# An attention block with experts on one core: scores in runs of three half tiles, values after one or two whole tiles

## The chip, the cores and the metric

The kernel runs on one core of one Trainium2 chip. The metric is the device time in microseconds of one execution of the whole program. Three runs of the kernel before gave 1203.56, 1205.45 and 1205.55 us; the median is 1205.45.

## The reference

Two sequences of 2048 tokens with 512 features go through causal attention with 16 query heads of 32 features that share one key head and one value head, a residual with a layer norm, a layer of eight experts of which each token takes two, and a second residual with a layer norm. The part that the change touches is this:

```python
qkv = jnp.einsum('bsd,ed->bse', x, Wqkv_w) + Wqkv_b
scores = jnp.einsum('bqhd,bkd->bhqk', q, k) * scale
scores = jnp.where(causal[None, None], scores, min_val)
attn = jax.nn.softmax(scores, axis=-1)
ctx = jnp.einsum('bhqk,bkd->bqhd', attn, v)
```

## The kernel before

The program loops over the two sequences. Each is worked in four stages g of four blocks q of 128 queries (q0 to q3, q4 to q7, q8 to q11, q12 to q15). A stage is attention, then the output product and the projections of the next stage, then the router and the experts.

A tile is one block of 128 queries against one block of 128 keys for all 16 heads, 2048 columns. Block q has q + 1 tiles, the diagonal one first, so a sequence has 136 tiles, numbered through (`TILES`, `FIRST[q]`, `LAST[q]`). Each engine has its own written order; semaphores join them:

- TensorE makes the scores of a tile in two halves of 1024 columns, two matmuls each (L1059). A half takes one of three places of a ring in PSUM. The fourth use of the ring takes the first place again and waits (`ring_free`) until the exponential has read the half that stood there, or, where a denominator stood there, until VectorE has transposed it (L798).
- ScalarE takes the exponential of each half into one of five buffers `prob` (L583). Before it writes a buffer again, it waits for the values and the addition, or the denominators, that read it.
- GpSimd masks the diagonal tile (L460). The first addition of a block waits for it.
- VectorE adds the tiles of a block up in `psum_k` (L749). The diagonal tile is taken in with the first addition; the last tile of q1 to q9 and the last two of q10 to q15 are left to TensorE (`BY_PE`); q0 and q1 have no addition.
- TensorE multiplies a tile's probabilities with the values (L1081, `times_values`): four column groups, two passes each, so eight passes, to a bank of PSUM that gathers the block. This is issued two tiles behind the scores (`LAG`).
- TensorE sums the rows of `psum_k` and of the tiles left to it into denominators (L1099, `denominators`), eight passes for each source: 24 passes where two tiles are left to it, 16 where one is. They are issued at the third tile of the next block (`DLAG`) and take a place of the ring. VectorE then transposes them (L798), takes reciprocals (L800) and scales the context (`normalise_context`).

In a stage but the first, the second half of the experts of the stage before (`finish_experts`, L1213 on TensorE, L822 to L832 on VectorE) comes behind the first tile's scores. VectorE starts its additions only behind that. Before the change the loop `attend_tiles` goes tile by tile: two halves of scores, then one tile's values, then denominators that are due. The list `ring_of` repeats this order, to give each use its place.

Behind the attention of a stage TensorE makes the output product (L949).

Of the kernel before, what the change touches and what calls it, by code (L numbers as in the profile page):

```python
# [35 lines left out]
P = 128  # L36
# [6 lines left out]
NG = S // BT  # L43
DC = D // P
TB = BT // P
NQ = S // P
HC = P // HD
HJ = H // HC
# [4 lines left out]
LAG = 2  # L53
# [7 lines left out]
FIRST = [TILES.index((q, q)) for q in range(NQ)]  # L61
LAST = [FIRST[q] + q for q in range(NQ)]
# [9 lines left out]
PV_ORDER = [t for q in range(NQ) for t in  # L72
            ([FIRST[q] + 1, FIRST[q]] + list(range(FIRST[q] + 2, LAST[q] + 1)) if q % TB
             else range(FIRST[q], LAST[q] + 1))]


def denominators_at(t):

    return [q for q in range(NQ) if LAST[q] + DLAG == t]


def ring_of(g):


    uses = []
    for t in range(FIRST[TB * g], LAST[TB * g + TB - 1] + 1):
        uses += [("scores", 2 * t), ("scores", 2 * t + 1)]
        uses += [("den", q) for q in denominators_at(t) if q >= TB * g]
    return uses


# [1 line left out]
RING_AT = [{use: n for n, use in enumerate(RING[g])} for g in range(NG)]  # L93
# [18 lines left out]
def build(nc, xT, x, wqkvT, bq, bvk, owT, ob, rT, w1, w2, w3, out):  # L112
    ctx = ExitStack()
    with ctx:
# [199 lines left out]
        def count(b, s, n):  # L314

            assert n > 0, (s, n)
            return b * GAIN[s] + n
# [15 lines left out]
        def score_half(g, u):  # L333

            return sc[:, RING_AT[g]["scores", u] % 3, :, :]
# [608 lines left out]
        def _(pe):  # L944
# [70 lines left out]
            with pe.Fori(0, B) as b:  # L1015
# [18 lines left out]
                def ring_free(g, n):  # L1034

                    if n >= 3:
                        kind, i = RING[g][n - 3]
                        if kind == "scores":
                            pe.wait_ge(exped, count(b, exped, i + 1))
                        else:  # L1040
                            pe.wait_ge(rden_ready, count(b, rden_ready, i + 1))

                def scores(t, g, shift):
                    q, k = TILES[t]
                    slot, at = (q % TB) // 2, (q % 2) * P
                    for half in range(2):
                        u = 2 * t + half
                        at_ring = RING_AT[g]["scores", u]
                        ring_free(g, at_ring)
                        if at_ring == 2:  # L1050
                            with pe.If(b > 0) if g == 0 else nullcontext():
                                pe.wait_ge(resid2, count(b - (g == 0), resid2, TB * ((g - 1) % NG) + (2 if g else TB)))
                                pe.sem_inc(waited_apart, 1)
                        for m in range(2):
                            c = 2 * half + m
                            if t == FIRST[q] and q % 2 == 0:
                                pe.wait_ge(stack_in[slot][c], count(b, stack_in[slot][c], 64 * (g + 1)))
                            dst = score_half(g, u)[:, m, :]
                            last = nc.tensor.matmul(dst, k_st[:, k * P:(k + 1) * P],  # L1059
                                                    q_st[slot][:, c * HJ:(c + 1) * HJ, at:at + P],  # L1060
                                                    start=True, stop=not shift)
                            for j in range(HJ if shift else 0):
                                h = c * HJ + j
                                last = nc.tensor.matmul(dst[:, j * P:(j + 1) * P],
                                                        minus_max[:, q % TB, h:h + 1].broadcast_to([P, P]),
                                                        ident[:, :], start=False, stop=(j == HJ - 1))
                        last.then_inc(scored, 1)

                def times_values(t):

                    q, k = TILES[t]
                    pe.wait_ge(exped, count(b, exped, 2 * (t + 1)))
                    if t == FIRST[q]:
                        pe.wait_ge(masked, count(b, masked, 2 * (q + 1)))
                    if t == PV_ORDER[FIRST[q]]:
                        if q % TB >= 2 or q // TB == 0 and q >= 2:
                            pe.wait_ge(ctx_out, count(b, ctx_out, q - 1))
                        elif q >= TB:
                            pe.wait_ge(resid2, count(b, resid2, TB * (q // TB - 1) + 3 + q % 2))
                    for c in range(HC):  # L1080
                        last = nc.tensor.matmul(top[q % 2][c * HD:(c + 1) * HD, :], v_sb[:, k, :],  # L1081
                                                prob[t % NP][:, c * BT:(c + 1) * BT],
                                                start=(t == PV_ORDER[FIRST[q]]), stop=(t == PV_ORDER[LAST[q]]))
                    last.then_inc(pv_done, 1)

                def denominators(q):

                    if FIRST[q] + 1 in ADDED:
                        pe.wait_ge(add_v, count(b, add_v, adds_until(LAST[q])))
                    if q % TB == TB - 1:  # L1090
                        pe.wait_ge(ctx_out, count(b, ctx_out, q))
                    else:
                        ring_free(q // TB, RING_AT[q // TB]["den", q])
                    parts = [prob[t % NP] for t in range(FIRST[q], LAST[q] + 1) if left_to_pe(t)]
                    if FIRST[q] + 1 in ADDED:
                        parts.append(psum_k[q % 2])
                    for n, src in enumerate(parts):
                        for c in range(HC):
                            last = nc.tensor.matmul(den_bank(q)[c * HD:(c + 1) * HD, :], ones[:, :],  # L1099
                                                    src[:, c * BT:(c + 1) * BT],  # L1100
                                                    start=(n == 0), stop=(n == len(parts) - 1))
                    last.then_inc(summed, 1)
# [14 lines left out]

                def attend_tiles(g, shift):
                    t0, t1 = FIRST[TB * g], LAST[TB * g + TB - 1]
                    for t in range(t0, t1 + 1):  # L1120
                        scores(t, g, shift)
                        if t == t0 and g:
                            finish_experts(g - 1)
                        if t - LAG >= t0:
                            times_values(PV_ORDER[t - LAG])
                        for q in denominators_at(t):
                            if q >= TB * g:
                                denominators(q)
                    for t in range(t1 - LAG + 1, t1 + 1):
                        times_values(PV_ORDER[t])  # L1130

# [164 lines left out]
```

## Time and profile before

| | us |
|---|---|
| median of three runs | 1205.45 |
| the profiled execution, its own time | 1201.47 |
| its span | 1199.3 |
| attention of the last stage of the first sequence, first score to last value | 424.0 to 561.5 |
| TensorE busy | 1099.2 |
| VectorE busy | 890.6 |
| ScalarE busy | 712.2 |
| mean granted TensorE clock, share of full | 0.978 |

The span is 2.2 us shorter than the profiled execution's time; the rest lies around it. Times of a row count from the span's start. PE is TensorE's matmuls, PEld its weight loads, DVE is VectorE, ACT ScalarE, POOL GpSimd. Busy shares are means over stages that have different limits, so a change is read from the stage that it is in.

### The profile page before, as it was taken

The page shows a single profiled execution, that of the slowest core. Times are in us where ns is not written, and L with a number is a line of the kernel's source. Part 1 is how long each engine was busy: PE and PEld are TensorE (multiplying, and loading weights), DVE is VectorE, ACT ScalarE, POOL GpSimd, SP SyncE. Part 2 cuts the span into 40 slices and gives each one's busy share as a digit, 9 for nine tenths or more (in the row PEclk, how much of TensorE's full clock was granted, in tenths as well). Part 3 has the DMA queues.
Part 4 walks back from the last instruction along what each step waited for, and adds up shares of the span by engine and source line. Part 5 has one row for each costly group of instructions (what it writes and reads, how often), then busy time and mean ns, then how long its engine had stood idle before and what let it go on. Part 6 is the DMA issues. An engine that isn't in the chain of part 4 may idle for free.

```text
span 1199.3 us, 18340 instructions
## 1 busy us (share of the span) xinstructions
PE 1099.2 (92%) x6080; PEld 525.2 (44%) x6080; DVE 890.6 (74%) x1095; ACT 712.2 (59%) x828; POOL 165.8 (14%) x153
## 2 busy tenths in 40 slices
PE   5489999998999999999989999999999999999976
PEld 4237433743335543333733743364333464333342
DVE  3176688669887589888677667875988767988856
ACT  4354568337884477887336347834688446788721
POOL 1250121102001012001004003020200101200000
PEclk9599999999999999999999999999999999999998
DMA  3991530063001432000154164016310143200000
GB/s 121 216 156 44 121 97 2 36 142 106 1 1 37 105 108 36 2 1 4 49 130 106 44 133 106 2 36 142 89 18 1 37 87 91 36 1 1 2 1 36
DMA packets 65678, 74.37 MB, mean 62 GB/s; under 512 B 14224, under 2 KB 48016, under 8 KB 65552
## 3 DMA queue, kind: packets, MB, share of 16 engines
q1 hardware_dynamic: 49968, 58.74, 19.0%
q0 software_dynamic: 13584, 11.54, 6.5%
q10 hardware_dynamic: 2000, 2.51, 0.7%
q8 instruction: 68, 1.11, 0.4%
q14 instruction: 58, 0.48, 0.1%
HBM read 25.58 MB, written 8.39 MB: 28 GB/s over the span
## 4 chain that ended last, share of the span: by engine, by line
PE 61%; DVE 22%; issue 8%; POOL 3%; ACT 2%; SPq 2%; DMA 1%; DVEq 0%; ACTq 0%; POOLq 0%
PE sc L1059 15%; DVE psum_k L749 13%; PE bank L1081 12%; PE sc L949 9%; PE sc L1198 7%; PE bank L949 7%; PE sc L1213 2%; PE sc L1099 2%; SPq L364 2%; ACT prob L583 2%; DVE stats L825 2%; PE bank L1099 2%; POOL prob L460 1%; DVE res L822 1%; PE sc L1144 1%
## 5 line engine op out<-in xcount | busy, mean ns | idle before, releaser
L583 ACT ACTIVATE prob<-sc 128x1024 f32<-128x1024 f32 x544 | 525.2, 1026 | 157.1 <-PE sc L1059 144.6
L749 DVE TENSOR_TENSOR psum_k<-psum_k,prob 128x2048 f32<-128x2048 f32 x170 | 395.6, 2327 | 5.1
L1059 PE MATMUL sc<-q_st,k_st 128*128 128x512 f32 x1088 | 334.0, 428 | 32.3 <-DMA q_st<-q_lo 11.7
L1059 PEld LDWEIGHTS sc<-q_st,k_st 128*128 128x128 f32 x1088 | 186.3, 191 | 280.2 <-ACT prob L583 178.3
L1081 PE MATMUL bank<-prob,v_sb 128*32 128x512 f32 x2176 | 290.7, 611 | 0.0
L460 POOL TENSOR_SCALAR_AFFINE_SELECT prob<-prob 128x1024 f32<-128x1024 f32 x64 | 88.7, 1423 | 596.5 <-ACT prob L583 596.5
L1198 PE MATMUL sc<-prob,w_sb 128*128 128x512 bf16 x512 | 123.0, 384 | 2.9 <-DVE prob L898 2.9
L749 DVE TENSOR_TENSOR psum_k<-prob 128x2048 f32<-128x2048 f32 x28 | 64.1, 2290 | 55.0 <-ACT prob L583 41.9
L1081 PEld LDWEIGHTS bank<-prob,v_sb 128*32 128x32 f32 x2176 | 44.0, 108 | 106.3 <-issue 90.7
L949 PE MATMUL bank<-q_st,wq_hi 128*128 128x512 f32 x240 | 81.0, 402 | 0.0
L615 ACT ACTIVATE prob<-sc 128x512 f32<-128x512 f32 x64 | 37.3, 597 | 69.8 <-PE sc L1198 69.7
L1198 PEld LDWEIGHTS sc<-prob,w_sb 128*128 128x128 bf16 x512 | 46.4, 99 | 66.3 <-issue 14.6
L949 PE MATMUL sc<-ow_hi,q_hi 128*128 128x512 f32 x128 | 52.3, 408 | 20.6 <-issue 20.6
L595 ACT ACTIVATE q_hi<-ctxn 128x512 fp32r<-128x512 f32 x32 | 20.3, 638 | 73.3 <-DVE ctxn L808 73.3
L817 DVE TENSOR_TENSOR q_lo<-ctxn,q_hi 128x512 fp32r<-128x512 f32 x32 | 50.6, 1590 | 12.3 <-ACT q_hi L595 12.1
L502 POOL TENSOR_TENSOR q_st<-res,q_st 128x2048 fp32r<-128x2048 f32 x7 | 33.1, 4733 | 144.0 <-ACT q_st L600 144.0
L898 DVE TENSOR_TENSOR prob<-sc,prob 128x512 f32<-128x512 f32 x64 | 42.1, 676 | 13.2 <-ACT prob L615 13.1
L949 PE MATMUL sc<-ow_lo,q_hi 128*128 128x512 f32 x128 | 50.6, 395 | 0.0
L949 PE MATMUL sc<-ow_hi,q_lo 128*128 128x512 f32 x128 | 50.6, 395 | 0.0
L949 PEld LDWEIGHTS bank<-q_st,wq_hi 128*128 128x128 f32 x240 | 45.7, 190 | 10.0 <-issue 0.2
L909 DVE TENSOR_TENSOR psum_k<-bank,prob 128x512 bf16<-128x512 f32 x64 | 42.4, 684 | 8.8 <-PE bank L1206 8.3
L545 ACT ACTIVATE q_hi<-bank,bq_sb 128x512 fp32r<-128x512 f32 x30 | 20.6, 689 | 45.9 <-PE bank L949 45.9
(127 smaller groups left out, 1004.9 us busy)
## 6 DMA issues: line engine op xcount, KB each, us to landing
q_st<-q_hi SPq DMA_DIRECT2D x128, 128.0 KB, 2.7
q_st<-q_lo SPq DMA_DIRECT2D x128, 128.0 KB, 2.7
res<-in_x SPq DMA_DIRECT2D x8, 1024.0 KB, 5.2
res<-ob_sb POOLq DMA_DIRECT2D x8, 1024.0 KB, 8.1
out_x<-res SPq DMA_DIRECT2D x32, 256.0 KB, 2.0
res<-in_xT SPq DMA_DIRECT2D x7, 1024.0 KB, 5.0
w_sb<-in_w POOLq DMA_DIRECT2D x8, 256.0 KB, 11.3
prob<-in_wqkvT ACTq DMA_DIRECT2D x4, 288.0 KB, 5.8
```

The source lines that it names most:

```text
L460: nc.gpsimd.affine_select(out=tile, in_=tile, compare_op=ALU.is_ge, fill=0.0, base=0, pattern=[[0, H // 2], [1, P]], channel_multiplier=-1 ...
L583: nc.scalar.activation(prob[t % NP][:, half * HW:(half + 1) * HW], score_half(q // TB, 2 * t + half).rearrange("p m n -> p (m n)"), ACT.Ex ...
L615: nc.scalar.activation(silu[e % 4], LOW[2 * (e % 3)], ACT.Silu).then_inc(silu_done, 1)
L749: nc.vector.tensor_tensor(acc[:, :], first[:, :], prob[t % NP][:, :], ALU.add).then_inc(add_v, 1)
L817: nc.vector.tensor_tensor(ctx_lo[:, :, toks], ctxn[:, :, toks], ctx_hi[:, :, toks].bitcast(F32), ALU.subtract).then_inc(ctx_low, 1)
L898: nc.vector.tensor_tensor(prod[e % 4], LOW[2 * (e % 3) + 1], silu[e % 4], ALU.mult).then_inc(prod_done, 1)
L909: nc.vector.tensor_tensor(hT[:, e, :], gate_bank(e)[:, :], prod[e % 4], ALU.mult).then_inc(h_done, 1)
L949: last = nc.tensor.matmul(dst, stationary[i][:, c, cols], moving[j][:, c, :], start=(c == 0 and n == 0), stop=(c == DC - 1 and n == 2))
L1059: last = nc.tensor.matmul(dst, k_st[:, k * P:(k + 1) * P], q_st[slot][:, c * HJ:(c + 1) * HJ, at:at + P], start=True, stop=not shift)
L1081: last = nc.tensor.matmul(top[q % 2][c * HD:(c + 1) * HD, :], v_sb[:, k, :], prob[t % NP][:, c * BT:(c + 1) * BT], start=(t == PV_ORDER[FI ...
L1099: last = nc.tensor.matmul(den_bank(q)[c * HD:(c + 1) * HD, :], ones[:, :], src[:, c * BT:(c + 1) * BT], start=(n == 0), stop=(n == len(par ...
L1198: last = nc.tensor.matmul(LOW[2 * (e % 3) + n], w[:, e, c, :], x1Tb[:, c, :], start=(c == 0), stop=(c == DC - 1))
```

## The change

TensorE's order in attention is the only thing that changes. The first tile of a stage is made as before. From then on scores are issued in runs of three halves. Behind a run come the values (two tiles behind, as before) and the due denominators of those tiles whose second half was made since the last run: one tile and two tiles in turn. The ring's list is made in the same new order. The same instructions run as before, as many of each, and the other engines' code is unchanged. From the second stage on, values of tiles t0 and later begin behind eight halves in place of six.

```diff
+def halves_of(g):
+    return range(2 * FIRST[TB * g], 2 * LAST[TB * g + TB - 1] + 2)
+
+def scored_by(g, u):
+    first, last = halves_of(g)[0], halves_of(g)[-1]
+    if u == first + 1:
+        return [u // 2]
+    if u != last and (u - first - 1) % 3:
+        return []
+    begin = first + 2 + 3 * ((u - first - 2) // 3)
+    return range((begin + 1) // 2 if begin % 2 == 0 else begin // 2, (u + 1) // 2)
+
 def ring_of(g):
     uses = []
-    for t in range(FIRST[TB * g], LAST[TB * g + TB - 1] + 1):
-        uses += [("scores", 2 * t), ("scores", 2 * t + 1)]
-        uses += [("den", q) for q in denominators_at(t) if q >= TB * g]
+    for u in halves_of(g):
+        uses.append(("scores", u))
+        uses += [("den", q) for t in scored_by(g, u) for q in denominators_at(t) if q >= TB * g]
     return uses
...
-                def scores(t, g, shift):
+                def scores(u, g, shift):
+                    t, half = divmod(u, 2)
                     q, k = TILES[t]
...
-                    for t in range(t0, t1 + 1):
-                        scores(t, g, shift)
-                        if t == t0 and g:
+                    for u in halves_of(g):
+                        scores(u, g, shift)
+                        if u == 2 * t0 + 1 and g:
                             finish_experts(g - 1)
-                        if t - LAG >= t0:
-                            times_values(PV_ORDER[t - LAG])
-                        for q in denominators_at(t):
-                            if q >= TB * g:
-                                denominators(q)
+                        for t in scored_by(g, u):
+                            if t - LAG >= t0:
+                                times_values(PV_ORDER[t - LAG])
+                            for q in denominators_at(t):
+                                if q >= TB * g:
+                                    denominators(q)
                     for t in range(t1 - LAG + 1, t1 + 1):
                         times_values(PV_ORDER[t])
```

Written out for q14 (tiles 105 to 119; s is a half, V a tile's values, D a block's denominators, | the end of a run):

```
before  s214 s215 V106 D13 | s216 s217 V105 | s218 s219 V107 | s220 s221 V108
after   s215 s216 s217 V106 D13 V105 | s218 s219 s220 V107 | s221 s222 s223 V108 V109
```

and for the start of q13 (tiles 91 to 104):

```
before  s186 s187 V92 D12 | s188 s189 V91 | s190 s191 V93
after   s185 s186 s187 V90 V92 D12 | s188 s189 s190 V91 | s191 s192 s193 V93 V94
```

## Rows read from the trace of the kernel before

**Rows 1.** The page: busy times; the chain that ended last; additions (busy us, mean ns).

```profile
PE 1099.2 (92%) x6080; PEld 525.2 (44%) x6080; DVE 890.6 (74%) x1095; ACT 712.2 (59%) x828; POOL 165.8 (14%) x153
...
PE 61%; DVE 22%; issue 8%; POOL 3%; ACT 2%; SPq 2%; DMA 1%; DVEq 0%; ACTq 0%; POOLq 0%
...
L749 DVE TENSOR_TENSOR psum_k<-psum_k,prob 128x2048 f32<-128x2048 f32 x170 | 395.6, 2327 | 5.1
```

**Rows 2.** Timeline, steady in q14: start us, duration us, engine, instructions [idle before <- releaser].

```profile
506.08 0.76 PEld L1059 LDWEIGHTS sc<-q_st,k_st 128*128 128x128 f32 x4 [0.84 <-ACT prob L583]
506.08 1.20 PE L1059 MATMUL sc<-q_st,k_st 128*128 128x512 f32 x4
506.85 1.94 ACT L583 ACTIVATE prob<-sc 128x1024 f32<-128x1024 f32 x2 [0.18 <-PE sc L1059]
...
507.21 1.07 PE L1081 MATMUL bank<-prob,v_sb 128*32 128x512 f32 x8
508.20 1.20 PE L1059 MATMUL sc<-q_st,k_st 128*128 128x512 f32 x4
508.97 1.02 ACT L583 ACTIVATE prob<-sc 128x1024 f32<-128x1024 f32 x1 [0.18 <-PE sc L1059]
```

**Rows 3.** Timeline of the same tile in windows so narrow that single starts show.

```profile
506.42 0.86 PE L1059 MATMUL sc<-q_st,k_st 128*128 128x512 f32 x3
...
506.88 0.40 PE L1059 MATMUL sc<-q_st,k_st 128*128 128x512 f32 x1
...
507.66 0.61 PE L1081 MATMUL bank<-prob,v_sb 128*32 128x512 f32 x4
```

**Rows 4.** Timeline, q12: exponentials back to back, and a score that waits for one.

```profile
439.56 1.94 ACT L583 ACTIVATE prob<-sc 128x1024 f32<-128x1024 f32 x2 [1.44 <-DVE psum_k L749]
...
440.64 0.50 PE L1059 MATMUL sc<-q_st,k_st 128*128 128x512 f32 x1 [0.25 <-ACT prob L583]
```

**Rows 5.** Timeline, the denominators of q13 at the third tile of q14.

```profile
493.66 2.29 DVE L749 TENSOR_TENSOR psum_k<-prob 128x2048 f32<-128x2048 f32 x1 [3.61 <-ACT prob L583]
494.01 1.06 PE L1081 MATMUL bank<-prob,v_sb 128*32 128x512 f32 x8
...
496.61 1.04 PE L1099 MATMUL sc<-psum_k,ones 128*32 128x512 f32 x8
...
497.58 0.77 PEld L1059 LDWEIGHTS sc<-q_st,k_st 128*128 128x128 f32 x4 [0.84 <-issue]
```

**Rows 6.** Waits for the transpose: waits view (us, times, longest); timeline behind q4, q9, q12.

```profile
PEld sc L1059 <- DVE rden L798: 28.3, 19, 3.1
...
163.29 1.89 PE L1059 MATMUL sc<-q_st,k_st 128*128 128x512 f32 x4 [2.19 <-DVE rden L798]
...
166.98 1.20 PE L1059 MATMUL sc<-q_st,k_st 128*128 128x512 f32 x4
...
322.41 1.21 PE L1059 MATMUL sc<-q_st,k_st 128*128 128x512 f32 x4 [0.41 <-DVE rden L798]
...
467.44 1.20 PE L1059 MATMUL sc<-q_st,k_st 128*128 128x512 f32 x4 [1.26 <-DVE rden L798]
```

**Rows 7.** Timeline, first stage: the second sequence's first six halves; the first sequence's DMA wait.

```profile
626.68 4.76 PE L1059 MATMUL sc<-q_st,k_st 128*128 128x512 f32 x12 [3.00 <-issue]
...
45.90 1.82 PE L1081 MATMUL bank<-prob,v_sb 128*32 128x512 f32 x8
...
53.33 0.76 PE L1059 MATMUL sc<-q_st,k_st 128*128 128x512 f32 x1 [4.95 <-DMA q_st<-q_lo]
```

**Rows 8.** Windows: busy PE, PEld, DVE, ACT, POOL, PEclk, DMA; then q15's end, timeline.

```profile
163.30:167.00 3.70, 3.70 (x13) 1.18 (x13) 3.54 (x4) 1.94 (x2) 0.00 (x0) 0.54 0.62 106
...
564.00:567.70 3.70, 3.70 (x20) 2.41 (x24) 3.70 (x1) 0.00 (x0) 3.44 (x1) 1.00 0.02 4
...
558.56 2.92 PE L1081 MATMUL bank<-prob,v_sb 128*32 128x512 f32 x24
...
563.95 0.49 PE L949 MATMUL sc<-ow_hi,q_hi 128*128 128x512 f32 x1 [2.46 <-issue]
```

More of the change, by code:

```diff
@@ L1041, in ring_free @@
                             pe.wait_ge(rden_ready, count(b, rden_ready, i + 1))
-                def scores(t, g, shift):
+                def scores(u, g, shift):
+                    t, half = divmod(u, 2)
                     q, k = TILES[t]
                     slot, at = (q % TB) // 2, (q % 2) * P
[L1046 to L1067, printed above, removed]
@@ new lines, in scores @@
+                    at_ring = RING_AT[g]["scores", u]
+                    ring_free(g, at_ring)
+                    if at_ring == 2:
+                        with pe.If(b > 0) if g == 0 else nullcontext():
+                            pe.wait_ge(resid2, count(b - (g == 0), resid2, TB * ((g - 1) % NG) + (2 if g else TB)))
+                            pe.sem_inc(waited_apart, 1)
+                    for m in range(2):
+                        c = 2 * half + m
+                        if t == FIRST[q] and q % 2 == 0:
+                            pe.wait_ge(stack_in[slot][c], count(b, stack_in[slot][c], 64 * (g + 1)))
+                        dst = score_half(g, u)[:, m, :]
+                        last = nc.tensor.matmul(dst, k_st[:, k * P:(k + 1) * P],
+                                                q_st[slot][:, c * HJ:(c + 1) * HJ, at:at + P],
+                                                start=True, stop=not shift)
+                        for j in range(HJ if shift else 0):
+                            h = c * HJ + j
+                            last = nc.tensor.matmul(dst[:, j * P:(j + 1) * P],
+                                                    minus_max[:, q % TB, h:h + 1].broadcast_to([P, P]),
+                                                    ident[:, :], start=False, stop=(j == HJ - 1))
@@ L1069, in times_values @@
+                    last.then_inc(scored, 1)
                 def times_values(t):
```

## The prediction

> **What bounds the kernel now.** I read the page's shares first, then the chain that ended last, then a steady stretch of the attention loop, then every place where that rhythm breaks. TensorE is busy for 92% of the span and holds 61% of the chain; VectorE 22% [rows 1]. In a steady stretch each tile (four score matmuls L1059, then eight value passes L1081) takes 2.12 us, 506.08 to 508.20. ScalarE needs 1.94 us for the tile's two exponentials and idles 0.18 waiting for scores; an addition takes VectorE 2.33 us, but not every tile has one [rows 1, 2]. So here TensorE sets the pace, with ScalarE 9% behind it.
>
> Inside the tile single instructions start so: scores 506.08, 506.42, then two more until 506.88; values 507.21, 507.66; next score 508.20 [rows 2, 3]. Neighbours of one kind follow after 0.23 us (scores) and, in a long train, 0.43 us for each four passes of values or denominators: eight last 1.04, four 0.61, and 8 value passes with 24 of the denominators take 494.01 to 497.58, which is 7 x 0.43 + 0.54 [rows 3, 5]. A change of kind costs more: 0.33 before the values instead of 0.23, 0.54 before the scores instead of 0.43, 0.34 for the second score instead of 0.23, 0.32 in all (with the 0.02 that the first value group takes beyond the rest). This is what the change addresses.
>
> Where TensorE waits in attention it waits mostly for VectorE: the third use of the ring behind a denominator needs the transpose L798 (28.3 us in the weight-load column, 19 times, longest 3.1). At 163.29 it waited 2.19, at 322.41 0.41, at 467.44 1.26 [rows 6]. Such places I call pins: VectorE (with GpSimd's masks ahead of it) sets their time.
>
> **The change part by part.**
> *Removed: switches.* No instruction is added or taken away. A pair of runs is six halves, that is three tiles: before 3 x 2.12 = 6.36 us, now 12 score matmuls, values of three tiles and two changes of kind, 6.36 - 0.32 = 6.04. All 136 tiles of a sequence go from 128 groups (after the first three tiles of each stage) to 85, so 43 switches x 0.32 x 2 = 28 us would go if nothing else ended late. That is the far end of the gain, not what I expect.
>
> *Added: waits inside a run.* The ring has three places, so the third half of a run needs the exponential of the third half of the run before. An exponential lasts 1.02 and two back to back 1.94, so they start 0.92 apart [rows 2, 4]. At 440.64 a blocked score starts 0.05 behind the end of the first of such a pair (439.56 + 1.02), and lasts 0.50 as the first behind a change of kind does, not 0.40, since its weights could not be loaded ahead [rows 4]. Take a run that starts at T after two tiles' values. Its first exponential starts at T + 0.77 (as 506.08 to 506.85), its third ends at T + 0.77 + 1.84 + 1.02 = 3.63. The next run (one tile's values between) starts at T + 2.58: 0.34 + 4 x 0.23 to the last score, 0.33 to the values, 0.99 through them. Its third half would start 1.03 later, T + 3.61, and may at T + 3.68. It is late by 0.07, and the lost preloading adds 0.1: about 0.15 a pair, taken once, because the run after two tiles' values has 0.8 us to spare. Net 0.32 - 0.15 = 0.17 for three tiles. The stall is a difference of two long sums, so I bound it by 0 and 0.3.
>
> *Moved: the denominators against the scores.* Behind q10, q13 and q14 the denominators now come after the first tile that reuses a buffer they read (two tiles are left to TensorE there), so its exponential waits for them. Before, its scores were issued behind them. If the last group of four passes starts at D, it ends at D + 0.61 (two such groups take 1.04 [rows 5]), the exponential at D + 1.66, and the scores that need its ring place may start at D + 1.71. Only one tile's values stand between, and they would let them start at D + 0.43 + 0.43 + 0.54 = 1.40: late by 0.3. The next half comes 0.57 later where its exponential takes 0.92 more: 0.35, and 0.1 for the lost preloading. That is some 0.73 each. For q1 (two tiles, both left to TensorE) the same. Bounds 0.3 to 1.0.
>
> *Moved: values behind a pin.* At a pin the time is VectorE's. Before, two halves of scores and one tile's values stood between denominator and pin; now three halves follow one another where the denominator ends its slot (q4, q5, q9, q12), and the values stand behind the pin. They were free in the idle time; they now cost 0.87 once for each last pin of a stage.
>
> The sum for one sequence, counted from the last pin of each stage (what is won before it is given back there):
> - q12 to q15: 41 tiles behind 467.44. The law above gives 41 x 2.12 + 2 x 2.6 for two denominators + 1.9 for the last two tiles' values = 94.0 us, the trace 558.56 + 2.92 - 467.44 = 94.0 [rows 6, 8]. 13.7 switches x 0.32 = -4.4; 11.7 waits x 0.15 = +1.8; two denominators +1.5; values behind the pin +0.9. Sum -0.2 to -0.4, I take -0.3.
> - q8 to q11: 19 tiles behind 322.41: -2.0, +0.8, one denominator +0.7, values +0.9: +0.4; the masks start a little earlier, I take +0.3.
> - q4 to q7: 11 tiles behind q5's denominator: -1.2, +0.5; the values behind it 0.87 less half a tile of scores already made (0.46): +0.4. Sum -0.3.
> - q0 to q3: beyond the third, the halves ahead of the first values are paced by exponentials: six take 4.76 us [rows 7], where free ones would take 3.0; two more such halves at 0.92, then two tiles' values: +0.3. One denominator +0.7, one wait +0.15, two switches -0.65. Sum +0.6.
> Together +0.3; two sequences +0.6. In the first sequence the scores of q2 wait for the stacked queries until 53.33, and the first values (1.82 us at the lower clock, 45.90) filled that time [rows 7]. They now stand behind it. A pin later in that stage can take most of it back: I take +0.4, bounds 0 and 1.8. Forecast +1.0 us: the profiled execution 1201.5 goes to 1202.5; on the median, 1206.5. About 0.2% (2.4 us) is what a measurement of this kernel can tell from no change.
>
> What hides the rest: the exponentials' later or earlier ends reach VectorE only where it idles (3.61 us before 493.66 [rows 5]); if that cover were gone, additions would bound at 2.33 a tile. Behind the last values of a stage 2.46 us pass before L949 starts at 563.95 [rows 8]; I leave that as it is.
>
> Consecutive scores start 0.23 apart although each load takes 0.19 and they use the same rows [rows 2, 3]. The Trainium skill, "TensorE: Matmul & The Clock Gate", "The mechanism", says a weight load overlaps matmuls in flight only when the row group differs. By it a run would gain nothing over pairs.
>
> **The rivals.**
> *The third half is not held* (faster). If the exponential ends 0.1 earlier against the scores than I reckon, the 0.15 goes at 21.7 pairs a sequence: -6.5 us for both, 1200.0. For it: the margin is 0.07 us. Against: the exponential's start and step repeat to 0.02 us.
> *The clock falls at a pin* (slower). With more done before a pin TensorE idles longer there: at 322.41 0.41 + one tile of scores already made 1.13 + values not yet made 1.0 + 0.5 won = 3.0 us; at 467.44 1.26 + 1.0 = 2.3. After the idle 2.19 at 163.29 the granted clock was 0.54 for 3.7 us, and four scores took 1.89 instead of 1.20; but after 2.46 at 563.95 it was 1.00 [rows 6, 8]. Price (166.98 - 163.29) - 2.12 = 1.6 us a fall: +3.2 for one place in both sequences, +6.4 for two: 1209.7 and 1212.9. The shortest idle behind which the rows show the fall is that of 2.19 us, and both places pass it.
> The Trainium skill, same page, "What's actually happening", has idleness take the clock to the lower level; the trace shows both outcomes.
> *The switches come off in full*: -28, 1177, if VectorE's pins and the ring gave way; nothing in rows 6 lets them.
> *It doesn't shorten a run* (the load rule): with equal spacing the changes of kind stay and the waits and moves are paid alone. The 26 switches that my sums count for a sequence are then not won, 8.2 us each, and it ends at 1223. The 0.23 spacing speaks against it.
>
> **How the numbers follow.** Forecast as reckoned 0.50; third half not held 0.20; clock falls at one or both pins 0.25; in full 0.02; nothing won 0.03. The range 1200 to 1213 takes in the first three. Within the forecast case the unknowns (stall 0 to 0.3, denominators 0.3 to 1.0, DMA 0 to 1.8) spread some 3 us either way: of its 0.50, 0.33 is same, 0.06 faster, 0.11 slower. Of the second 0.16 is faster, 0.04 same; the third is slower but for 0.01. Faster 0.24, same 0.38, slower 0.38.
>
> **What would show it.** Right: in q14's steady part runs of six score matmuls, tile values one and two, three tiles in 6.2 us; an exponential ending just before every second run's third half; a wait of some 3 us at q10's pin and over 2 at q13's; ScalarE's waits for scores grouped instead of 0.18 each. Wrong: three tiles in 6.04 (no hold) or 6.4 and more (a hold in every run); no new wait behind q13's and q14's denominators; the last values of q15 more than 2 us earlier against the pin of q13; a granted clock under 1.00 behind either pin puts the time with the slower rival.

## The result, and the profile after

| | before | after |
|---|---|---|
| median of 20 runs each | 1205.65 (1200.52 to 1212.27) | 1215.7 (1204.75 to 1223.13) |
| the profiled execution, its own time | 1201.47 | 1220.64 |
| its span | 1199.3 | 1218.5 |
| mean granted TensorE clock of that execution | 0.978 | 0.961 |

The change makes the kernel slower: the ratio to before is 1.0069, with an interval of 1.0048 to 1.0091 (it is reckoned over the fast runs alone; the two medians of the table give 1.0083). The measured 1215.7 is 9.2 above the forecast and 2.7 above the upper end of the range. The page after, against [rows 1] (busy times, the clock in 40 slices, the chain):

```profile
PE 1100.4 (90%) x6056; PEld 541.0 (44%) x6080; DVE 890.9 (73%) x1095; ACT 701.4 (58%) x828; POOL 166.4 (14%) x153
...
PEclk9599999999999999999999999999999999999978
...
PE 69%; DVE 14%; issue 8%; ACT 4%; POOL 2%; SPq 2%; DMA 1%; ACTq 0%; DVEq 0%; POOLq 0%
```

Nothing in it says where 19.2 us of span went: VectorE's additions left the chain (22% to 14%), TensorE took their share, and slices of 30 us are too coarse for the clock.

The order itself came as drawn. The timeline of q14's steady part, to read against [rows 2, 3] (start, duration, engine, instructions, idle before and releaser):

```profile
510.61 1.65 PE L1075 MATMUL sc<-q_st,k_st 128*128 128x512 f32 x6
511.37 2.86 ACT L600 ACTIVATE prob<-sc 128x1024 f32<-128x1024 f32 x3 [0.18 <-PE sc L1075]
512.19 1.92 PE L1097 MATMUL bank<-prob,v_sb 128*32 128x512 f32 x16
514.04 1.65 PE L1075 MATMUL sc<-q_st,k_st 128*128 128x512 f32 x6
514.82 4.69 ACT L600 ACTIVATE prob<-sc 128x1024 f32<-128x1024 f32 x5 [0.59 <-PE sc L1075]
515.63 1.06 PE L1097 MATMUL bank<-prob,v_sb 128*32 128x512 f32 x8
516.62 1.84 PE L1075 MATMUL sc<-q_st,k_st 128*128 128x512 f32 x6
517.73 0.30 PEld L1075 LDWEIGHTS sc<-q_st,k_st 128*128 128x128 f32 x2 [0.35 <-ACT prob L600]
...
520.25 1.65 PE L1075 MATMUL sc<-q_st,k_st 128*128 128x512 f32 x6
```

A run starts at 510.61, 514.04 and 516.62. With two tiles' values it takes 3.43, with one 2.58, and the run at 516.62 lasts 1.84 instead of 1.65: its third half waited for ScalarE (the 0.35 in the weight-load line). The pair of runs that starts at 514.04 ends at 520.25: 6.21 us for three tiles, with this wait in it; 6.19 was reckoned, 6.36 was the price before. (The pair before it, from 510.61 to 516.62, had no wait and took 6.01.)

Where did the time go? The attention stages (first score to last value) and what stands between them, from the starts and ends in the timelines of both kernels:

| | before | after | difference | forecast |
|---|---|---|---|---|
| q0 to q3, first / second sequence | 44.91 / 26.64 | 47.36 / 27.70 | +2.45 / +1.06 | +1.0 / +0.6 |
| q4 to q7 | 70.19 / 70.24 | 70.63 / 69.90 | +0.44 / -0.34 | -0.3 |
| q8 to q11 | 104.29 / 104.04 | 104.36 / 104.32 | +0.07 / +0.28 | +0.3 |
| q12 to q15 | 137.45 / 137.76 | 138.91 / 139.54 | +1.46 / +1.78 | -0.3 |
| last value of q3 to the next stage | 55.99 / 56.06 | 54.99 / 54.38 | -1.00 / -1.68 | 0 |
| of q7 | 56.41 / 56.73 | 58.16 / 56.84 | +1.75 / +0.11 | 0 |
| of q11 | 56.80 / 56.83 | 58.90 / 58.76 | +2.10 / +1.93 | 0 |
| of q15 (to the second sequence / to the end) | 65.20 / 64.32 | 69.17 / 69.13 | +3.97 / +4.81 | 0 |

Attention holds 7.2 us of the 19.2; the other 12.0 lie where the change moved nothing. Windows of both kernels say why (busy PE, PEld, DVE, ACT, POOL, then the granted clock, DMA share, GB/s). TensorE's clock has two levels here, full (1.00) and half; a number between them is the mean over the window, and a place behind which the lower level shows is called fallen, or a fall, from here on. First after, behind the ends of q7, q11 of the second sequence, and q15, and behind the pins of q13 and q10:

```profile
211.10:215.50 4.40, 4.36 (x12) 3.35 (x12) 4.40 (x2) 0.00 (x0) 3.40 (x1) 0.61 0.02 4
...
953.90:958.00 4.10, 4.10 (x12) 2.93 (x12) 3.58 (x1) 0.00 (x0) 3.03 (x1) 0.66 0.01 4
...
571.50:580.00 8.50, 7.57 (x28) 3.63 (x32) 3.65 (x1) 0.00 (x0) 3.10 (x1) 0.60 0.41 127
...
473.10:476.50 3.40, 3.40 (x13) 1.29 (x14) 3.24 (x4) 1.02 (x1) 0.00 (x0) 0.62 0.66 114
...
325.40:328.80 3.40, 3.40 (x20) 1.64 (x24) 3.24 (x4) 2.02 (x3) 0.00 (x0) 1.00 0.00 0
```

The same three stage ends before:

```profile
209.30:213.70 4.40, 4.40 (x28) 2.65 (x28) 3.91 (x1) 0.00 (x0) 3.37 (x1) 1.00 0.02 4
...
942.90:947.00 4.10, 4.10 (x24) 2.54 (x28) 3.93 (x1) 0.00 (x0) 3.38 (x1) 1.00 0.03 8
...
564.00:572.50 8.50, 8.50 (x48) 5.15 (x49) 6.37 (x5) 0.04 (x1) 3.44 (x1) 1.00 0.43 125
```

Behind the end of q7 TensorE started 12 matmuls of the output product in 4.4 us after, 28 before, at a granted clock of 0.61 against 1.00. Behind q15 the mean was 0.60 over 8.5 us. Five of eight stage ends fell after and none before; so did q13's pin in both sequences, but not q10's. The pin behind q4's denominators fell in both kernels and both sequences, so it makes no difference here.

What TensorE waited for just ahead of these windows (timeline: q10's pin, q13's pin, end of q15):

```profile
325.38 0.73 PE L1075 MATMUL sc<-q_st,k_st 128*128 128x512 f32 x2 [2.37 <-DVE rden L815]
...
473.05 0.73 PE L1075 MATMUL sc<-q_st,k_st 128*128 128x512 f32 x2 [1.89 <-DVE rden L815]
473.71 1.78 PE L1097 MATMUL bank<-prob,v_sb 128*32 128x512 f32 x8
475.43 2.52 PE L1075 MATMUL sc<-q_st,k_st 128*128 128x512 f32 x6
...
571.52 0.50 PE L966 MATMUL sc<-ow_hi,q_hi 128*128 128x512 f32 x1 [2.76 <-issue]
...
574.22 0.79 PE L966 MATMUL sc<-ow_hi,q_hi 128*128 128x512 f32 x1 [0.92 <-issue]
```

The pins waited 2.37 and 1.89 us, not 3.0 and 2.3; the shorter one fell and the longer one did not. Eight value passes at 473.71 take 1.78 us where a full clock gives 1.06, and the six scores behind them 2.52 instead of 1.65. The end of q15 idled 2.76 after and 2.46 before [rows 8].

### The profile page after: what moved, and what is told of

Read it like the earlier page. It is cut to its first block, busy times and chain, and to the rows that moved or that the text cites. A ratio compares the mean times of both kernels' runs of the same rounds, so it can differ in the third digit from the quotient of the medians.

```text
span 1218.5 us, 18300 instructions
## 1 busy us (share of the span) xinstructions
PE 1100.4 (90%) x6056; PEld 541.0 (44%) x6080; DVE 890.9 (73%) x1095; ACT 701.4 (58%) x828; POOL 166.4 (14%) x153
## 4 chain that ended last, share of the span: by engine, by line
PE 69%; DVE 14%; issue 8%; ACT 4%; POOL 2%; SPq 2%; DMA 1%; ACTq 0%; DVEq 0%; POOLq 0%
PE sc L1075 18%; PE bank L1097 16%; PE sc L966 10%; PE sc L1215 7%; PE bank L966 7%; DVE psum_k L766 6%; ACT prob L600 3%; PE sc L1115 2%; PE sc L1230 2%; SPq L381 2%; PE bank L1115 2%; POOL prob L477 2%; PE sc L1161 1%; DVE stats L842 1%; PE bank L1223 1%
## 5 line engine op out<-in xcount | busy, mean ns | idle before, releaser
L600 ACT ACTIVATE prob<-sc 128x1024 f32<-128x1024 f32 x544 | 514.1, 1033 | 172.2 <-PE sc L1075 138.7
L1075 PE MATMUL sc<-q_st,k_st 128*128 128x512 f32 x1088 | 330.2, 430 | 52.1 <-DVE rden L815 16.5
L1097 PE MATMUL bank<-prob,v_sb 128*32 128x512 f32 x2176 | 277.1, 611 | 0.0
L1215 PE MATMUL sc<-prob,w_sb 128*128 128x512 bf16 x488 | 118.6, 383 | 5.3 <-DVE prob L915 2.9
L1097 PEld LDWEIGHTS bank<-prob,v_sb 128*32 128x32 f32 x2176 | 53.3, 109 | 125.9 <-issue 97.3
L966 PE MATMUL sc<-ow_hi,q_hi 128*128 128x512 f32 x128 | 55.2, 431 | 20.5 <-issue 17.8
L966 PE MATMUL sc<-ow_lo,q_hi 128*128 128x512 f32 x128 | 53.7, 419 | 0.0
L966 PE MATMUL sc<-ow_hi,q_lo 128*128 128x512 f32 x128 | 53.3, 416 | 0.0
L966 PEld LDWEIGHTS bank<-q_st,wq_hi 128*128 128x128 f32 x240 | 45.7, 190 | 10.2 <-issue 0.2
L966 PE MATMUL bank<-q_st,wq_lo 128*128 128x512 f32 x120 | 47.6, 397 | 0.0
```

Source lines behind the costliest of these rows:

```text
L600: nc.scalar.activation(prob[t % NP][:, half * HW:(half + 1) * HW], score_half(q // TB, 2 * t + half).rearrange("p m n -> p (m n)"), ACT.Ex ...
L966: last = nc.tensor.matmul(dst, stationary[i][:, c, cols], moving[j][:, c, :], start=(c == 0 and n == 0), stop=(c == DC - 1 and n == 2))
L1075: last = nc.tensor.matmul(dst, k_st[:, k * P:(k + 1) * P], q_st[slot][:, c * HJ:(c + 1) * HJ, at:at + P], start=True, stop=not shift)
L1215: last = nc.tensor.matmul(LOW[2 * (e % 3) + n], w[:, e, c, :], x1Tb[:, c, :], start=(c == 0), stop=(c == DC - 1))
```

## The experiments

The experiments ran in four groups, each on a chip of its own with runs of the kernel before beside them, whose medians were 1206.96 us (the same kernels again, filled stage ends), 1208.36 (the switches alone, both versions with filled stage ends of the last experiment), 1205.89 (last tiles, both versions without them) and 1207.17 (pins). A ratio is to the runs of its own group; a difference between two groups carries theirs, up to 2.5 us.

**Does the same kernel give the same clock?** Both kernels again as they are, no edit.

> The kernel before once more, to see how its time and its mean granted TensorE clock go together from run to run. Theory (the clock): at equal order of work the time falls and rises with the clock, some 10 us for 0.01 of it (half of 1219 us x 0.01 lost twice over), clocks near 0.976 to 0.98 and 1201 to 1205 us. Rival (the order itself costs the time): the clock tells nothing, and even its lowest clocks don't reach 1214 us.

> The kernel with the change once more, beside the kernel before on the same chip. Theory (the clock): 8 to 12 us slower than before, its clocks near 0.961 to 0.970; plotted against the clock its runs lie on the line of the kernel before, within 3 us. Rival (the order costs it): its runs lie 8 us or more above that line.

Measured: before 1206.92 (12 runs, 1200.38 to 1212.21), ratio 0.9986 [0.996, 1.0012]; the change 1218.78 (8 runs, 1204.62 to 1221.04), ratio 1.0076 [1.0035, 1.0118]. The new profile of before is another picture than the first: four of its eight stage ends fell, after idle times as long as in the profile where none did. Timeline and window of again_before at the end of q15, and its window at q13's pin:

```profile
569.55 0.78 PE L949 MATMUL sc<-ow_hi,q_hi 128*128 128x512 f32 x1 [2.74 <-issue]
...
569.60:574.00 4.40, 4.40 (x12) 3.34 (x12) 3.62 (x1) 0.00 (x0) 3.07 (x1) 0.61 0.11 10
...
473.00:476.50 3.50, 3.50 (x24) 1.43 (x23) 3.34 (x4) 2.78 (x3) 0.00 (x0) 1.00 0.58 101
```

Two windows and the lines ahead of them show how much that is a matter of the execution. They are the same place, the end of q11 in the first sequence, in the first profile of before and in again_before:

```profile
369.67 0.50 PE L949 MATMUL sc<-ow_hi,q_hi 128*128 128x512 f32 x1 [2.44 <-issue]
...
369.70:374.10 4.40, 4.40 (x28) 2.67 (x32) 3.98 (x1) 0.00 (x0) 3.43 (x1) 1.00 0.03 7
...
373.58 0.49 PE L949 MATMUL sc<-ow_hi,q_hi 128*128 128x512 f32 x1 [2.46 <-issue]
...
373.60:378.00 4.40, 4.40 (x16) 3.07 (x20) 3.99 (x1) 0.00 (x0) 3.44 (x1) 0.66 0.02 4
```

The same code idles 2.44 us and keeps its clock, and idles 2.46 us and falls.

In again_after five stage ends fell, q13's pin in one sequence, and in both sequences the pin behind q8's denominators, which had waited 1.17 us and kept its clock in the first profile of the change. Now it waited 1.99 us (timeline and window, first sequence):

```profile
302.32 0.73 PE L1075 MATMUL sc<-q_st,k_st 128*128 128x512 f32 x2 [1.99 <-DVE rden L815]
...
302.30:306.00 3.70, 3.68 (x14) 1.78 (x15) 3.54 (x4) 1.38 (x2) 0.00 (x0) 0.66 0.60 105
```

Every run has a mean clock beside its time. Over the 31 runs of before beside these the two go together: 10.5 us for a hundredth of mean clock (a straight line through them). That line puts before at 1201.7 for a clock of 0.978; the 20 runs of the change lie on a line of 9.3 us, which puts it at 1203.4. At a clock of 0.978 the change thus costs 1.7 us, but none of its runs had so high a clock; at 0.970, where both kernels have runs, the two lines are 0.8 apart. Single runs scatter by 1.3 us around either line, so the change costs some 0 to 2 us at equal clock, where +1.0 was forecast. The mean clock of these runs was 0.9725 and 0.9645, and 0.008 x 10.5 = 8.4 us; their mean times, 1207.5 and 1216.0, are 8.5 apart. The clock goes with nearly all of it.

**Idle stage ends filled.** Ten dummy matmuls behind the last values of a stage, in both kernels. The falls there should vanish, and if they are the loss, the gain is larger for the change.

```diff
                     for t in range(t1 - LAG + 1, t1 + 1):
                         times_values(PV_ORDER[t])
+                    for _ in range(10):
+                        nc.tensor.matmul(LOW[5], k_st[:, 0:P], k_st[:, 0:BT], start=True, stop=True)
```

> The change, and behind the last values of each attention stage ten matmuls of 512 columns (2.3 us) on constant data whose result nobody reads, so that TensorE is busy where it idled 2.7 us before the output product. Theory (five of the seven idle times there brought the clock down for 3.4 us each, 1.7 us a piece): the falls behind L966 at stage ends vanish, and it is 5 to 9 us faster than the change alone, within 4 us of the kernel before. Rival (the falls follow something else, or cost nothing): same time as the change alone or 2 us a stage slower (16 us), if the filler isn't hidden.

> Control: the kernel before with the same ten matmuls at each stage end. Its trace shows no fall there, so theory (clock) expects the same time within 2 us, or up to 3 us faster if some runs do have falls there; rival (the filler itself costs): 10 us or more slower.

Measured: warm_after 1205.41 (ratio 0.9979 [0.9955, 1.0003]), warm_before 1202.0 (0.9953 [0.9931, 0.9975]); 12 runs each. The change gains 10.3 us against the 1215.7 of its 20 runs (13.4 against again_after), before gains 4.9 against again_before; both are more than expected. No stage end falls in either profile. Timeline of warm_after at the end of q15:

```profile
562.00 2.59 PE L1149 MATMUL sc<-k_st 128*128 128x512 f32 x10
...
565.08 0.49 PE L966 MATMUL sc<-ow_hi,q_hi 128*128 128x512 f32 x1 [0.49 <-issue]
```

The idle time is 0.49 instead of 2.76. The output product starts 3.0 us behind the last values; without dummies it starts 2.4 to 3.1 behind them at the ends of q7, q11 and q15 in the four profiles so far, so the dummies cost nothing that shows. Most of the change's loss was the clock: 3.4 us are left between the two, with mean clocks of 0.9744 and 0.9784, and 0.004 x 10.5 = 4.2 is all of that.

**The switches alone.** In both kernels the exponentials of q4 to q15 are cut to half their width and the additions to a quarter (that part of the computation is left out), so that neither holds TensorE. Both have the ten dummy matmuls at the stage ends too.

```diff
-activation(prob[t % NP][:, half * HW:(half + 1) * HW], ...
+activation(prob[t % NP][:, half * HW:half * HW + (HW if q < TB else 512)], ...
-tensor_tensor(acc[:, :], first[:, :], prob[t % NP][:, :], ALU.add)
+tensor_tensor(acc[:, 0:W if q < TB else 512], ...
```

> The kernel before with the ten matmuls at stage ends; from the second stage on ScalarE takes the exponential of only 512 of a half's 1024 columns and VectorE adds only 512 of a tile's 2048 (that part of the computation is left out), so neither the ring nor VectorE holds TensorE back. It is the base of the pair with free_after. Theory: TensorE sets the pace at 2.12 us a tile as before, its waits for the transpose are gone, and it is some 10 to 20 us faster than with full exponentials and additions.

> The same shortened exponentials and additions under the order of the change. Theory (a switch costs 0.32 us and its saving is real, but is given back at the ring and at VectorE's pins): three tiles take 6.04 us without a wait in the run, and it is 20 to 26 us faster than free_before (about 40 switches a sequence in the stages without first one, 0.32 each). Rival (the switches save nothing, or TensorE itself gives it back): within 5 us of free_before.

Measured: 1174.32 (ratio 0.9734 [0.9697, 0.9772]) and 1150.75 (0.9544 [0.9507, 0.958]), 4 runs each: the change wins 23.6 us. (free_before itself is 27.7 us under warm_before, more than the 10 to 20 expected.) By stage it wins 1.83, 3.53 and 5.89 us in the first sequence for 8, 13 and 19 switches saved: 0.23 to 0.31 each, just under the 0.32 reckoned. Timeline of free_after in q14:

```profile
498.41 1.65 PE L1075 MATMUL sc<-q_st,k_st 128*128 128x512 f32 x6
500.00 1.92 PE L1097 MATMUL bank<-prob,v_sb 128*32 128x512 f32 x16
501.85 1.65 PE L1075 MATMUL sc<-q_st,k_st 128*128 128x512 f32 x6
503.43 1.07 PE L1097 MATMUL bank<-prob,v_sb 128*32 128x512 f32 x8
504.43 1.66 PE L1075 MATMUL sc<-q_st,k_st 128*128 128x512 f32 x6
```

Three tiles take 504.43 - 498.41 = 6.02 us and no run is held (6.04 was reckoned). So the idea works, and what cancels it in the real kernel comes from ScalarE and VectorE, the ring's hold and the pins; the pair takes both away at once and doesn't say how much each of them cancels. This refutes the rival that a run saves nothing.

**Is it the last tiles of a stage?** Perhaps runs of three halves ahead of a stage's end make its fall more frequent. The change gets the old pairs for the last six to eight runs of each stage; before gets the new runs of three for the last four.

```diff
+# after_oldtail
+RUNS = [[3]*2 + [2]*6, [3]*12 + [2]*7, [3]*22 + [2]*8, [3]*34 + [2]*6]
+# before_newtail
+RUNS = [[2]*3 + [3]*4, [2]*19 + [3]*4, [2]*35 + [3]*4, [2]*51 + [3]*4]
```

> The change, but the last six tiles of each stage in the order before (two halves of scores, one tile's values). At an equal clock the steps of the forecast put it within 2 us of the change. Theory A (what TensorE does in the last 12 us ahead of a stage's end decides how often the clock falls in the idle time there): mean granted clock up from 0.964 towards 0.969 to 0.972, 4 to 7 us faster than the change. Theory B (the falls at stage ends follow the idle time alone, whatever ran ahead): mean clock near 0.964, 1214 to 1218 us.

> The mirror: the order before, but the last six tiles of each stage in runs of three halves. At an equal clock within 2 us of the kernel before. Theory A: mean clock down from 0.973 towards 0.966 to 0.969, 4 to 7 us slower than the kernel before. Theory B: mean clock 0.972 to 0.974, the time of the kernel before.

Measured: after_oldtail 1223.37 (6 runs, ratio 1.0136 [1.0096, 1.0176], mean clock 0.963), above what either theory expected, so the old end restores nothing: in its profile six of eight stage ends fell, q3's in both sequences among them, where the change had none. It is even some 6 us slower than the change at the same clock (its line gives 1217.4 at 0.963), which I can't explain in full. before_newtail 1213.12 (12 runs, 1.0045 [1.0019, 1.007], clock 0.9688), 7 us slower. That would fit (the line of before gives 1211.3 at 0.9688), and five of its eight stage ends fell, but its profile shows another difference: the end of q15 idles about twice as long as in any other kernel here (5.70 and 5.33 us), for nothing that the profile shows. Timeline of before_newtail:

```profile
570.85 0.79 PE L979 MATMUL sc<-ow_hi,q_hi 128*128 128x512 f32 x1 [5.70 <-issue]
```

The pair doesn't settle it: one half speaks against the tail as the cause, the other is spoilt by a second difference.

**Is it the pins?** Dummy matmuls ahead of the pins behind the denominators of q4, q8, q9 and q12 (q9's is the prediction's pin of q10, q12's that of q13; in before, q4, q8 and q12); pins_ends has those at the stage ends too.

```diff
+if g and at_ring >= 3 and RING[g][at_ring - 3][0] == "den":
+    qd = RING[g][at_ring - 3][1]
+    for _ in range({4: 2, 8: 1, 9: 2, 12: 2}.get(qd, 0)):
+        for n in range(HC):
+            nc.tensor.matmul(top[(qd + 1) % 2][n * HD:n * HD + HD - E, :], rT_sb[:, 0, E:HD],
+                             k_st[:, 0:BT].bitcast(F32), start=False, stop=False)
 ring_free(g, at_ring)
```

> The change in its own order; where the third half behind the denominators of q4, q8, q9 and q12 waits for VectorE's transpose, TensorE first makes one (q8) or two sets of value-like matmuls with zero weights that add nothing (0.87 us a set), so it is busy where it idled 1.2 to 2.5 us. Stage ends are left as they are. Theory P (the falls at the pins cost the change some 3 to 5 us): 1210 to 1215 us against 1216 to 1219 for the change, mean clock 0.967 to 0.970. Theory E (stage ends are all of it): 1216 to 1219 us, clock 0.964.

> The same, and the ten matmuls at each stage end. With those alone the change took 1205.4 us. Theory P: 2 to 4 us less, 1201 to 1203.5 us, clock 0.977 to 0.980. Theory E: 1205 us as before.

> Its counterpart: the order before, with the ten matmuls at stage ends and the zero matmuls where the third ring place behind the denominators of q4 (two sets), q8 and q12 (one each) is waited for. If the clock accounts for what the forecast missed, this and pins_ends_after differ by what the forecast gave, the change 0 to 3 us slower (forecast +1.0); 1199 to 1202 us. If the order itself costs more, the difference is 5 us or over.

Measured, 12 runs each: pins_after 1202.25 (ratio 0.9958 [0.9932, 0.9984], clock 0.9764), pins_ends_after 1199.9 (0.9938 [0.991, 0.9966], clock 0.9802), pins_ends_before 1199.95 (0.9938 [0.9915, 0.9961], clock 0.9806). Filled pins alone take 13.5 us from the 1215.7 (16.5 from again_after), where theory P expected 1210 to 1215 us. Timeline and windows of pins_after: the dummies and the pin behind them, then q13's pin, the end of q15, and the clock behind the last two:

```profile
318.74 1.92 PE L1069 MATMUL bank<-k_st,rT_sb 128*24 128x512 f32 x16
321.19 0.73 PE L1081 MATMUL sc<-q_st,k_st 128*128 128x512 f32 x2 [0.53 <-DVE rden L815]
...
467.29 0.73 PE L1081 MATMUL sc<-q_st,k_st 128*128 128x512 f32 x2
...
564.22 0.49 PE L966 MATMUL sc<-ow_hi,q_hi 128*128 128x512 f32 x1 [2.85 <-issue]
...
467.20:470.70 3.50, 3.45 (x24) 1.66 (x24) 3.31 (x5) 2.00 (x3) 0.00 (x0) 1.00 0.65 113
...
566.00:570.00 4.00, 4.00 (x31) 1.46 (x29) 1.80 (x1) 0.00 (x0) 1.25 (x1) 1.00 0.28 73
```

The stage end idles 2.85 us, no less than before, and yet doesn't fall; in the whole profile one of eight does. So the idle length at a stage end alone doesn't decide, and filling other gaps, such as the one 95 us earlier, went with fewer falls there. Why, this doesn't show: either what ran long before a gap counts, or only the moment at which it comes does, for a filled pin also moves all that stands behind it. In the first profile of the change four pins had fallen (those behind q4's and q12's denominators, in both sequences), at 1.6 us each 6.4 us; the other 7 came from places that were not filled.

With both kinds of place filled the two orders are equal to 0.05 us, at equal clock. That the order itself costs 5 us or more is refuted. Their attention stages differ, change less before, by -0.57, -0.09, +0.31, -0.36 us in the first sequence and +0.60, -0.01, -1.09, -0.35 in the second (in the -1.09 before had a fall of the clock). The forecast had +1.0, -0.3, +0.3, -0.3 and +0.6, -0.3, +0.3, -0.3.

**Can the order win?** Two steps on the change. ahead: a denominator is followed at once by the values that otherwise stand behind the pin. runs: besides, the length of each run is chosen so that a denominator's place and the pin suit the run. Each with the filled stage ends (warm) and without (cold).

```diff
 denominators(q)
+while AHEAD[g] and valued <= t - LAG + 1:
+    times_values(PV_ORDER[valued])
+    valued += 1
+# runs_warm and runs_cold, here the last stage
+RUNS[3] = [3,3,4,4,3,1,4,3,3,3,2,2] + [3]*19 + [2,3,2,3,3,3,3,3]
```

> The change with the ten matmuls at stage ends, and from the second stage on the next tile's values are issued right behind the denominators, ahead of the run that waits for the transpose (which tile's values stand behind a pin was step three of the sum, 0.9 us for each stage). Theory: the idle time at the pins of q10 and q13 falls from 2.4 and 1.9 us by 0.9 each, with it the falls of the clock there; 4 to 8 us faster than the change with the ten matmuls alone, 1197 to 1201 us, at or below the kernel before. Rival (the values are not what is late there): no difference beyond 1 us.

> As ahead_warm, but the lengths of the runs are chosen stage by stage (1 to 4 halves) so that denominators don't follow a reused buffer's tile and the pins find work: reckoned by the same steps as the forecast (ring, buffers, VectorE's chain), 3.5 us shorter in each of the last three stages of a sequence than the order before, about 20 us for the program: 1180 to 1186 us. If the steps are wrong where runs are uneven, it lies near ahead_warm, 1197 to 1201.

> The change with the next tile's values right behind the denominators (the pins' part alone, without the ten matmuls at stage ends). With them it took 1196.7 us. Theory (stage ends cost the change some 10 us through the clock, the pins some 3): 1204 to 1209 us, between the change and the kernel before or level with the latter, mean clock 0.966 to 0.970. Rival (the pins' falls are the larger part): 1199 to 1203 us.

> The chosen run lengths without the ten matmuls at stage ends; with them it took 1182.1 us. Theory (the filler is worth its clock falls, as much as between the change with and without it): 1188 to 1195 us, mean clock 0.968 to 0.974. Rival (its stage ends keep the clock by themselves): 1181 to 1184 us.

Measured: ahead_warm 1196.68 (8 runs, one of them at 2148.77 us and not in the ratio; 0.9912 [0.988, 0.9944]), 8.7 us under warm_after; ahead_cold 1204.97 (12 runs, 0.9972 [0.9948, 0.9997]); runs_warm 1182.13 (6 runs, 0.9808 [0.9778, 0.9838]); runs_cold 1185.13 (6 runs, 0.9812 [0.9777, 0.9847]). With the values ahead the two pins wait 1.53 and 1.02 us (timeline of ahead_warm):

```profile
320.19 1.66 PE L1078 MATMUL sc<-q_st,k_st 128*128 128x512 f32 x6 [1.53 <-DVE rden L818]
...
465.32 1.66 PE L1078 MATMUL sc<-q_st,k_st 128*128 128x512 f32 x6 [1.02 <-DVE rden L818]
```

Run lengths and values ahead together take 3.2 to 5.4 us from each attention stage but the first of a sequence, against warm_before (in the 5.4 warm_before had a fall). So time of the size of the switches can be won in the real kernel: 19.9 us between warm_before and runs_warm, of which ahead_warm already had 5.3, beside the 23.6 of the free pair. runs_warm is the best version, some 2% under before; without the dummies it keeps all but 3 us of that, less lost than its theory had (1188 to 1195 us), and three of eight stage ends fell in its profile.

## Why the prediction was wrong, and where it was right

**The switch.** Right: 6.21 us for three tiles against 6.19, 6.02 against 6.04 where nothing holds. The hold of the third half was there in every second run, as the forecast had it and its rival had not. The Trainium skill, "TensorE: Matmul & The Clock Gate", "The mechanism", lets a weight load overlap only matmuls of another row group; the free pair's 23.6 us speak against it, as the 0.23 spacing did.

**The denominators.** Right in kind and, nearly, in size. Timeline of after behind q13's denominators:

```profile
505.30 1.04 PE L1115 MATMUL sc<-psum_k,ones 128*32 128x512 f32 x8
506.16 1.04 PE L1097 MATMUL bank<-prob,v_sb 128*32 128x512 f32 x8
506.49 1.94 ACT L600 ACTIVATE prob<-sc 128x1024 f32<-128x1024 f32 x2 [3.59 <-PE sc L1115]
...
507.56 0.73 PE L1075 MATMUL sc<-q_st,k_st 128*128 128x512 f32 x2 [0.36 <-ACT prob L600]
508.48 1.20 PE L1075 MATMUL sc<-q_st,k_st 128*128 128x512 f32 x4 [0.18 <-ACT prob L600]
```

ScalarE waits 3.59 us until the denominators have read its buffer, and the scores are late by 0.36 where 0.3 was reckoned; the next half is late by 0.18 where 0.35 was.

**Values behind a pin, and the sums by stage.** Right within 0.75 us in five of eight stages. The two q12 to q15 came out 1.8 and 2.1 above, and each holds one fall at q13's pin; at the 1.6 of [rows 6] what is left is -0.1 and +0.2, for a forecast of -0.3. The first stage's +2.45 is in part a clock that stayed low longer, and it is not steady: in again_before and again_after that stage takes 45.24 and 45.20 us. (The forecast's own terms for a first stage, 0.3 + 0.7 + 0.15 - 0.65, add up to 0.5 and not 0.6.) The idle times at the pins were over-estimated by 0.6 and 0.4.

**The clock.** This is the step that failed, and the sentence is "Behind the last values of a stage 2.46 us pass before L949 starts at 563.95 [rows 8]; I leave that as it is." The rows of one profile showed no fall there [rows 8], and I took that for a property of the place. It was chance: the same kernel's second profile has four falls in eight such places. The sum thus put the clock at the stage ends at nothing. The rival on the clock named the right mechanism and had two places a sequence, 3.2 or 6.4 us; the stage ends that it left out hold most of what separates the two first profiles, 12.0 of 19.2 us. In the first profile of the change, of 96.0 us at half clock (before 52.7), the stage ends hold 23.9 (0), the first stage 37.5 (30.7), q13's pins 6.8 (0) and the end of the kernel 17.5 (11.8); q4's pins and the start of the second sequence hold 10.2 in both. The range's upper end stood on 6.4 and missed. Its condition, that 2.19 us of idle time is the shortest with a fall behind it, didn't hold either: q13's pin fell after 1.89, while q10's kept its clock after 2.37.

A weakness of the base goes with it: the profiled execution, 1201.47 us at 0.978, was a good one of its kernel, whose mean clock was 0.9725. The forecast adds its +1.0 to the median, so this didn't shift it, but rows of a good execution show fewer falls than the median run has.

**What stays open.** Why the change's stage ends fall more often, five of eight in both of its profiles against none and four (four profiles are few, but the mean clocks of the timed runs, 0.9645 and 0.9725, say the same). Old last tiles didn't cure it, filled pins nearly did, filled stage ends did by removing the place. That the chip takes in what came long before a gap fits these runs but was not shown. That the moment at which a gap comes decides fits them as well, with the end of q11 above, and no run was made to part the two. The 5.70 us of before_newtail, the 0.92 at 574.22 and the shorter idle at q3's end after the change (1.75 and 0.82, where before has 2.62 and 2.52) are "issue": nothing in the profile ends them.

## What to carry to other kernels

Before a sum on a kernel that TensorE sets, list every place where TensorE idles about 2 us or more, look at the granted clock behind each in several profiles, and price a fall at all of them, also where the change moves nothing. Compare orders at equal clock (the mean clock beside each run's time, or gaps filled with dummy work), else the clock hides what the order did. A saving on the bounding engine shows only when what stands next (here the ring's hold and VectorE's pins) is placed for it: about as many saved switches gave 0 us at a fixed run length and, with the values ahead of the pins, 19.9 at chosen ones.

## What the runs showed of the hardware

The granted clock is not repeatable. The kernel before had mean clocks of 0.963 to 0.979 in its runs but one (0.835, at 1279.04 us), the change 0.958 to 0.976; a hundredth went with 10.5 us of 1205, and with that most of the spread between runs of one kernel is told (what is left around the line is 1.3 us). It fell after idle times of 1.89 and 1.99 us, and not after others of 2.37, 2.44 and 2.85. A fall shows as a mean granted clock of 0.54 to 0.66 over the next four microseconds, and costs 1.6 to 2.1 us, twice that at the end of q15, where it lasted longer. The Trainium skill, "TensorE: Matmul & The Clock Gate", "What's actually happening", has the lower level as the state of an idle engine, and every fall named here stands behind idle time; which gap brings it on, the length of the gap doesn't tell.

Changing from full-array score matmuls to column-tiled value matmuls and back costs 0.23 to 0.31 us here, reckoned from whole stages of the free pair. Between the last values of a stage and the output product lie 2.3 to 3.1 us at the ends of q7, q11 and q15 (but for before_newtail) and 0.8 to 2.9 at q3's, in which TensorE's next matmul waits for nothing that the profile shows; dummy matmuls put there run inside that time.
